# Graph attention layer in the tail: the last octet's scores and softmax earlier, the last iteration's pooling and decoding a step earlier in another PSUM bank

## The reference

```python
h = x @ w_lin + b_lin
dense[n, pos] = h[src of edge]                        # n x 32 x 64, mask[n, pos]
xb = mab(dense, dense, enc_*, mask)                   # attention, + residual, + relu(ff)
xp = relu(xb @ pma_lin_w + pma_lin_b)
p  = mab(seed, xp, pma_*, mask)                       # one query a node
dd = mab(p, p, dec_*)
out = relu(nan_to_num(dd))
return layernorm(x + out)
```

## Time and profile before

| | |
|---|---|
| time, median of 3 runs | 4012.61 us (4012.59 to 4014.58) |
| the profiled execution | 4014.11 us, span 4012.3 us |
| busy PE, DVE, POOL, ACT | 78%, 76%, 74%, 41% of the span |
| mean granted clock of TensorE | 0.923 |
| last gather issued | 3948.2 to 3949.2 us |
| last instruction ends | 4012.3 us |

### The profile page before, as it was taken

One profiled execution on the slowest core, in us unless ns is written; L12 is line 12 of the kernel. 1 busy time (PEld: TensorE's weight loads), 2 busy tenths in 40 slices (PEclk: granted clock), 3 DMA queues, 4 the chain that ended last, 5 costly groups with the idle time before them and its releaser, 6 DMA issues.

```text
span 4012.3 us, 111968 instructions
## 1 busy us (share of the span) xinstructions
PE 3111.6 (78%) x30804; PEld 2000.9 (50%) x30804; DVE 3057.7 (76%) x7192; ACT 1663.4 (41%) x3006; POOL 2979.5 (74%) x3145
## 2 busy tenths in 40 slices
PE   7877887877777778777787787787877777877777
PEld 5544554554545445545454455454554554545443
DVE  6877877877778768777787787777877877778876
ACT  3443443444434434444444344344444443434443
POOL 6777777777777777777777777777777777777772
PEclk8999998999989989999899899998999999999898
DMA  6333333333333333333333333333333333333331
GB/s 215 90 90 90 90 91 90 90 91 89 90 90 89 91 90 89 90 90 90 90 89 90 90 89 91 90 90 90 89 91 90 90 90 90 90 90 89 87 109 34
DMA packets 186843, 369.25 MB, mean 92 GB/s; under 512 B 66610, under 2 KB 119002, under 8 KB 186090
## 3 DMA queue, kind: packets, MB, share of 16 engines
q0 software_dynamic: 150080, 307.11, 28.8%
q1 hardware_dynamic: 29802, 45.03, 3.5%
q10 hardware_dynamic: 6208, 8.40, 0.7%
HBM read 347.48 MB, written 16.32 MB: 91 GB/s over the span
## 4 chain that ended last, share of the span: by engine, by line
POOL 66%; issue 24%; PE 6%; DVE 2%; DMA 1%; POOLq 1%; SPq 0%; ACT 0%; DVEq 0%
POOL gathered L620 66%; DMA gathered<-node_table,idx 1%; PE ps L788 1%; PE ps L726 1%; PE ps L738 1%; PE ps L770 1%; PE ps L801 0%; DVE windows L1135 0%; PE ps L815 0%; PE ps L831 0%; PE ps L762 0%; POOLq L131 0%; DMA node_table<-gathered 0%; PE ps L689 0%; DVE probs_diag L1382 0%
## 5 line engine op out<-in xcount | busy, mean ns | idle before, releaser
L620 POOL DMA_INDIRECT gathered<-node_table,idx x3093 | 2934.4, 949 | 943.3 <-issue 938.7
L726 PE MATMUL ps<-ident,gathered 128*128 128x128 f32 x3128 | 583.5, 315 | 458.2 <-DMA gathered<-node_table,idx 452.3
L726 PEld LDWEIGHTS ps<-ident,gathered 128*128 128x128 f32 x3128 | 485.1, 203 | 796.0 <-issue 732.2
L852 ACT ACTIVATE h_apart<-ps 64x512 f32<-64x512 f32 x782 | 462.3, 591 | 448.9 <-PE ps L726 355.3
L925 ACT ACTIVATE qT<-ps,cols 128x512 f32<-128x512 f32 x391 | 268.8, 687 | 854.3 <-PE ps L726 754.4
L1306 DVE SCALAR_TENSOR_TENSOR xb<-ps,cols,h 128x512 f32<-128x512 f32 x391 | 292.1, 747 | 417.6 <-PE ps L788 412.4
L1382 DVE STREAM_TRANSPOSE probs_diag<-probs 32x512 f32<-32x512 f32 x784 | 549.0, 700 | 18.4
L738 PE MATMUL ps<-probs_diag,gathered 128*64 128x128 f32 x6256 | 462.4, 292 | 107.4 <-issue 106.1
L788 PE MATMUL ps<-h,ff_diag 128*128 128x512 f32 x782 | 484.0, 705 | 76.0 <-DVE h L1262 75.5
L738 PEld LDWEIGHTS ps<-probs_diag,gathered 128*64 128x64 f32 x6256 | 373.9, 169 | 276.8 <-issue 259.1
L852 ACT ACTIVATE xp_rows<-ps 128x512 f32<-128x512 f32 x391 | 233.4, 597 | 601.0 <-PE ps L762 419.6
(11 more groups left out here) (205 smaller groups left out, 3287.2 us busy)
## 6 DMA issues: line engine op xcount, KB each, us to landing
windows<-win_table SPq DMA_DIRECT2D x8960, 2.8 KB
gathered<-node_table,idx POOLq DMA_INDIRECT x3093
windows<-win_table ACTq DMA_DIRECT2D x2944, 2.8 KB
node_table<-gathered SPq DMA_DIRECT2D x24, 384.0 KB, 2.8
out_rows<-rows SPq DMA_DIRECT2D x5, 416.0 KB
win_table<-in_dst SPq DMA_DIRECT2D x1, 1716.0 KB
win_table<-in_src SPq DMA_DIRECT2D x1, 1716.0 KB
rows<-in_x SPq DMA_DIRECT2D x2, 640.0 KB, 5.1
```

Source lines behind the costliest of these rows:

```text
L620: pool.indirect_dma_start(out=gathered[:, s.slot(0, RING), t * ROW:(t + 1) * ROW], out_offset=None, in_=table, in_offset=bass.IndirectOffs ...
L726: mm = pe.transpose(ps[:, bank, p * P:(p + 1) * P], gathered[:, s.slot(0, RING), lo:lo + 2 * ROW - 2:3], ident[:, :])
L852: return nc.scalar.activation(o, i, ACT.Copy)
```

## The change

`alone()` is true in step 391 of the written-out tail, `alone(1)` in 392, `alone(2)` in 393. In step 391 the scores of batch 195 are issued directly behind attend(387) on PE instead of at the end of the step. DVE's mask, add, maximum and difference of that batch move from step 392 to step 391, behind the second half of the transposes and ahead of the statistics; ACT's exp moves from the end of 392 to the end of 391; the share-out and the transposes move from step 393 to step 392. For iteration 97 alone, everything from the seed mask to y is a step sooner in program order (395 to 402 instead of 396 to 403), and its transposed weights, pooling and decoding results are in bank B_Q, which the turn of an octet used before; its pooling has no wait for `y_ok` then. The looped steps and all other written-out steps have the same instructions in the same order. The same code of the batch's softmax now stands in functions (`masked`, `shared_out`, `from_top`, `first_half`).

```diff
+LAST_SOONER = {L_SEED: 1, L_SEED_T: 1, L_WEIGHTS: 1, L_POOL: 1, L_DEC1: 1, L_DEC2: 1, L_OUT: 1, L_Y: 1}
...
+    def sooner(self, lag):
+
+        if self.looped or lag not in LAST_SOONER:
+            return 0
+        last = (self.octets - 1) // 4 * 4
+        return LAST_SOONER[lag] if self.at - lag + LAST_SOONER[lag] == last else 0
...
-        return self.group * (PERIOD // 4) + (self.at - lag) // 4
+        return self.group * (PERIOD // 4) + (self.at - lag + self.sooner(lag)) // 4
...
+    def alone(self, after=0):
+        return not self.looped and self.at == self.octets + after
+
     def has_iteration(self, lag):
-        return (self.at - lag) % 4 == 0 and (self.looped or 0 <= self.at - lag < self.octets)
+        at = self.at - lag + self.sooner(lag)
+        if at % 4 or self.looped:
+            return at % 4 == 0
+        moved = LAST_SOONER.get(lag, 0) and at == (self.octets - 1) // 4 * 4 and not self.sooner(lag)
+        return 0 <= at < self.octets and not moved
...
+        def pool_bank(s, lag):
+            return B_Q if not s.looped and s.iteration(lag) == ITS - 1 else B_POOL
+
+        def seedT_of(s, lag):
+            return ps[:, pool_bank(s, lag), P:2 * P]
+
+        def fin_of(s, lag):
+            return ps[:, pool_bank(s, lag), 2 * P:3 * P]
...
                     mm.then_inc(av_ps, 1)
+                if s.alone():
+                    scores(s)
                 if s.has_iteration(L_DEC1):
-                    fin_op(s, L_DEC1, pooled_ok, ps_fin[0:D, :], pooled, ident)
+                    fin_op(s, L_DEC1, pooled_ok, fin_of(s, L_DEC1)[0:D, :], pooled, ident)
...
                     wait(pe, weights2_ok, s.iteration(L_POOL) + 1)
-                    wait(pe, y_ok, s.iteration(L_POOL))
+                    if pool_bank(s, L_POOL) == B_POOL:
+                        wait(pe, y_ok, s.iteration(L_POOL))
...
-                        mm = pe.matmul(ps[DEG * c:DEG * c + DEG, B_POOL, :],
+                        mm = pe.matmul(ps[DEG * c:DEG * c + DEG, pool_bank(s, L_POOL), :],
...
-                if s.has_batch(L_SCORES):
...
+                if s.has_batch(L_SCORES) and not s.alone():
+                    scores(s)
+
+            def scores(s):
+                wait(pe, p_norm, s.batch(L_SCORES))
+                wait(pe, q_sb, s.octet(L_SCORES - 2))
+                wait_apart(pe, h_parted, s.octet(L_SCORES - 2) * 2, pe_passed)
...
-                if s.has_batch(L_SOFTMAX):
-                    wait(act, s_diff, s.batch(L_SOFTMAX) + 1)
+                if s.alone() or s.has_batch(L_SOFTMAX) and not s.alone(1):
+                    wait(act, s_diff, s.batch(L_SOFTMAX - s.alone()) + 1)
                     nc.scalar.activation(ps_scores, ps_scores, ACT.Exp).then_inc(p_exp, 1)
...
+                if s.has_batch(L_SOFTMAX) and not s.alone(1):
+                    masked(s, L_SOFTMAX)
+                if s.has_batch(L_NORM) and not s.alone(2):
+                    shared_out(s, L_NORM)
+                if s.alone(1):
+                    shared_out(s, L_NORM - 1)
                 if s.has(L_H2):
...
+                if s.has_batch(L_SOFTMAX) and not s.alone(1):
+                    from_top(s, L_SOFTMAX)
+                if s.has_batch(L_NORM) and not s.alone(2):
+                    first_half(s, L_NORM)
+                if s.alone(1):
+                    first_half(s, L_NORM - 1)
...
-                if s.has_batch(L_NORM):
-                    to_diagonal(s, pr, QUADS // 2, QUADS)
+                if s.has_batch(L_NORM) and not s.alone(2):
+                    to_diagonal(s, L_NORM, QUADS // 2, QUADS)
+                if s.alone(1):
+                    to_diagonal(s, L_NORM - 1, QUADS // 2, QUADS)
+                if s.alone():
+                    masked(s, L_SOFTMAX - 1)
+                    from_top(s, L_SOFTMAX - 1)
                 if s.has_iteration(L_Y):
                     y_stats(s)
```

More of the change, by code:

```diff
@@ L1227, in step @@
                     y_rows(s)
[L1228 to L1243, removed]
@@ L1291, in step @@
                     wait(dve, fin_ps, m * 6 + 3)
-                    V.scalar_tensor_tensor(pvec[:, :], ps_fin[0:D, :], c_("bff2"), hid1[:, :], ALU.add, ALU.max
+                    V.scalar_tensor_tensor(pvec[:, :], fin_of(s, L_DEC2)[0:D, :], c_("bff2"), hid1[:, :], ALU.add, ALU.max
                                            ).then_inc(pvec_ok, 1)
@@ L1377, in step, with masked @@
                     act_rows_of(s)
-            def to_diagonal(s, pr, first, last):
+            def masked(s, lag):
+                n = s.batch(lag)
+                dve.wait_ge(s_ps, n + 1)
+                V.tensor_tensor(
+                    empty[:, :].rearrange("p (o t j) -> p o t j", o=2, j=DEG),
+                    ps_iota.unsqueeze(1).unsqueeze(1).broadcast_to((P, 2, OCT, DEG)),
+                    count_slot[:, bass.ds(n * 16, 16)].rearrange("p (o t) -> p o t", o=2).unsqueeze(3).broadcast_to(
+                        (P, 2, OCT, DEG)), ALU.is_ge).then_inc(mask_ok, 1)
+                if s.has_iteration(lag):
+                    m = s.iteration(lag)
+                    V.tensor_copy(count_seed[:, bass.ds(m, 1), :].rearrange("p m a -> p (m a)"), ps_counts[:, 0:QUADS])
+                    V.tensor_scalar(nonempty[:, bass.ds(m, 1)], ps_counts[:, QUADS:QUADS + 1], 0.0, None, ALU.is_gt
+                                    ).then_inc(counts_read, 1)
+                dve.wait_ge(mask_ok, n + 1)
+                V.scalar_tensor_tensor(ps_scores, empty[:, :].rearrange("p (h n) -> p h n", h=2), MASKED, ps_scores,
+                                       ALU.mult, ALU.add).then_inc(s_sb, 1)
@@ new lines, in shared_out @@
+            def shared_out(s, lag):
+                pr = probs[:, s.slot(lag, 4) // 2, :]
+                n = s.batch(lag)
+                dve.wait_ge(p_exp, n + 1)
+                V.tensor_reduce(total[:, :].rearrange("p (h t) -> p h t", h=2), ps_slots, AX_X, ALU.add
+                                ).then_inc(p_sum, 1)
+                dve.wait_ge(p_sum, n + 1)
+                V.reciprocal(share[:, :], total[:, :]).then_inc(p_share, 1)
+                dve.wait_ge(p_share, n + 1)
+                V.tensor_tensor(pr.rearrange("p (h t j) -> p h t j", h=2, j=DEG), ps_slots,
+                                share[:, :].rearrange("p (h t) -> p h t", h=2).unsqueeze(3).broadcast_to(
+                                    (P, 2, OCT, DEG)), ALU.mult).then_inc(p_norm, 1)
@@ L1380, in to_diagonal, with first_half @@
+            def first_half(s, lag):
+                n = s.batch(lag)
+                dve.wait_ge(p_norm, n + 1)
+                wait(dve, av_ps, s.octet(lag + 2))
+                to_diagonal(s, lag, 0, QUADS // 2)
+            def to_diagonal(s, lag, first, last):
+                pr = probs[:, s.slot(lag, 4) // 2, :]
                 for q in range(first, last):
                     lo = DEG * q
-                    V.transpose(probs_diag[lo:lo + DEG, s.slot(L_NORM, 4) // 2, :, lo:lo + DEG],
+                    V.transpose(probs_diag[lo:lo + DEG, s.slot(lag, 4) // 2, :, lo:lo + DEG],
```

75 lines of the change are left out of this document (39 added, 36 removed).

## The result

The changed kernel takes 4019.87 us (median of 22 runs, 4016.16 to 4022.9), the kernel before 4013.68 beside it (22 runs, 4011.7 to 4017.46). The ratio is 1.0016, with a 95% interval of 1.001 to 1.0021: 6.2 us slower, where 3.3 were forecast. It is within the 0.2% that was taken for no change, and 0.4 us above the upper end of the stated range.

What follows compares the result with a forecast made beforehand. Bound: POOL's pace of issuing gathers in the loop, DVE's queue in the tail. Order 3.5, plus clock 1.4, less decode 1.65, is 3.3 us slower: 4015.9 us against the median 4012.61, range 4010.5 to 4019.5.

Steps and rivals of the forecast that it cites:

- Scores in step 391, "1.83 late": Step 391 on PE: the moved scores wait for the norm and hold up back and seed; ff(387) starts 1.83 us late.
- PE's idle stretch of 3.6 us, DEC1 4.5 late: Step 392 on PE: first decoding transpose waits for DVE's pooling until 3970.40, 4.5 us later; PE idles 3.6.
- What sets ff(388): Step 392: PE has back and seed done at 3972.08 but waits for h2; ff(388) starts at 3972.77.
- The order costs 3.5 at the full clock: Steps 391 to 394: xb(388) 4.88 us late, 1.35 back in steps 393 and 394, so 3.5 lost.
- That adds 1.4 us; ... so no more is added.: Behind PE's 3.6 us wait: clock falls for 5.6 us, slowing back, seed and ff; 1.4 us more.
- the stated bound of 2.9: Upper bound of the clock term in steps 392 and 393: 2.9 us if pma and attend are still slow.
- rival of a later recovery: Step 393: clock returns one step later, pma, attend and part of back slow, another 1.5 to 2.5 us, 4018; 13%.
- Part 2, 1.65 back: Last decode: pooling(97) follows the OUT matmul without waiting for y of 96, winning 1.65 us; bounds 0 to 2.2.
- The detour: Decode of iteration 96: transpose of seed weights and its product stand ahead of pvec, costing 0.47 us together.
- The sum: Whole tail: 3.5 for the order plus 1.4 for the clock less 1.65 for the decode, 3.3 us slower.
- Different time up to the last gather: Ahead of the tail: a sign that the prediction is wrong, putting the cause outside the tail; no size given.

Runs made afterwards that it cites:

- e14: Changed kernel with unused extra matmuls filling both PE waits (four in step 391, seven in 392), third run: 1.7 us over before, ratio 1.0005.
- e6: Changed kernel, but in step 391 DVE does the pooling of iteration 95 ahead of the moved softmax instructions: ratio 1.0001 against before.
- e5: Changed kernel with unused extra matmuls filling both PE waits (four in step 391, seven in 392), first run: ratio 1.0003 against before.
- e4: The changed kernel again, unaltered, for a second trace: ratio 1.0007 against before.
- e9: The changed kernel again, unaltered, for a third trace: ratio 1.0004 against before.
- e2: Kernel before with only the scores and softmax of the last batch moved, iteration 97 and its bank as before: ratio 1.0011 against before.
- e8: Kernel before with only the scores and softmax of the last batch moved, second run: ratio 1.0006 against before.
- e16: The changed kernel again, unaltered, for a fourth trace: 5.2 us over before, ratio 1.0013.
- e3: Changed kernel with eleven unused extra matmuls in step 392, filling only PE's second wait, ahead of DEC1: ratio 1.0013 against before.
- e1: Kernel before with only iteration 97 a step sooner and in the other bank, softmax as before: ratio 0.9996 against before.
- e7: Kernel before with only iteration 97 a step sooner and in the other bank, second run: ratio 0.9986 against before.
- e10: Changed kernel with unused extra matmuls filling both PE waits (four in step 391, seven in 392), second run: ratio 0.9998 against before.
- e15: Softmax as before, iteration 97 a step sooner in the other bank, its pooling two steps sooner, second run: 4.1 us below before, ratio 0.999.

## Why the prediction was right in direction and short in size

- **Scores in step 391, "1.83 late".** Right: ff(387) is 5.88 behind attend(387), before 4.03, 1.85 late.
- **PE's idle stretch of 3.6 us, DEC1 4.5 late.** Right: 3.55 in the changed kernel's first trace, the transpose 4.53 late.
- **What sets ff(388).** The text put PE's idle stretch in bold; its own sum then let ff(388) wait for h2, by 0.7. The sum was right, and the idle stretch by itself costs nothing at the full clock: with the clock up, ff(388) waits 0.63 for h2 (e14), and e6, which releases DEC1 2.8 earlier, has h2(388) no earlier.
- **The order costs 3.5 at the full clock.** Right: 29.83 less 26.38 is 3.45 (e5). xb(388) is 4.92 late (e14), where 4.88 was forecast, and steps 393 and 394 give back 1.48, where it was 1.35: xb to xb is 6.05 and 6.17.
- **The step that failed: "That adds 1.4 us; ... so no more is added."** The fall behind the second wait was rightly foreseen. Its size was taken from one low stretch, put at 5.6 us behind a restart (5.8 by the 0.77 of the earlier trace rows), and only waits of 3.5 us and more were looked at. The runs show three things in its place. First, the term is 1.56, 5.05, 5.16 and 4.67 in four traces (the time to xb(390) less 29.83), so the stated bound of 2.9 was too low. Second, the wait of 2.15 that the moved scores make can bring a fall too, and the prediction gave it no price: of eight traces with that wait the clock is down ahead of the scores in two (e4, e9), falls within them in three (e2, e6, e8) and just behind them in one (e16), and stays up in two (the first trace, e3). Third, the second stretch ends 5.0 to 5.2 us behind the restart in three traces (the first, e2, e8), but 8.7 to 11.6 behind it in four (e4, e6, e9, e16), over pma(388) and attend(389). The rival of a later recovery (13%) came closest, with 4018.
- **The trace of before could have warned.** From 3000 to 3950 it has 18 waits of 2.0 to 3.1 us for gathered rows. Behind 11 of them the next ff takes 1.02, behind the 7 others 1.42 to 1.92. One of each:

```profile
3217.47 1.09 PE L726 MATMUL ps<-ident,gathered 128*128 128x128 f32 x4 [2.41 <-DMA gathered<-node_table,idx]
3218.36 1.91 PE L788 MATMUL ps<-h,ff_diag 128*128 128x512 f32 x2
...
3944.78 0.69 PE L726 MATMUL ps<-ident,gathered 128*128 128x128 f32 x4 [2.38 <-DMA gathered<-node_table,idx]
3945.31 1.02 PE L788 MATMUL ps<-h,ff_diag 128*128 128x512 f32 x2
```

- **Part 2, 1.65 back.** Measured 1.0 to 1.1 in e1 and e7, 1.1 to 1.5 in the changed kernel. The detour itself was rightly priced for the full clock. From the first matmul of DEC2 to pvec it was 0.47 (3991.47 to 3991.94), and in e10, where the clock is still up, it is 0.93, 0.46 more:

```profile
6466.05 0.43 PE L878 MATMUL ps<-hid,p_ff 64*64 64x128 f32 x2 [0.45 <-ACT hid L941]
...
6466.98 0.33 DVE L1294 SCALAR_TENSOR_TENSOR pvec<-ps,cols,hid 64x128 f32<-64x128 f32 x1
```

What was off is again the clock. In the first trace it is down ahead of that matmul and the same way takes 1.33 (3996.15 to 3997.48), 0.86 more. Every trace has a fall in the decode of 96 that lasts to the end, and its place matters: it comes 9.1 us behind xb(390) in before, e4 and e9, where the gain is 1.5, and 7.9 to 8.1 behind it in e1, e7 and the first trace, where it is 1.0 to 1.3.

- **The sum.** 3.45 + 1.56 - 1.26 = 3.75 in the trace that was taken of the result, and 3.45 + 5.0 - 1.4 = about 7.0 in the three others. A median of 6.2 over 22 runs is what a mixture of these would give; the two traces on such chips have tails of 59.63 and 62.90 and times of 4017.77 and 4021.02, 3.3 apart in both. e14 and e16 show in times that it is the clock. How often each case occurs I can't say from four traces.
- **"Different time up to the last gather".** Not seen: attend(387) starts at 3956.42 and 3953.83 in the two traces of before and at 3955.97 and 3955.90 in the two of the changed kernel on chips of this speed. By so few a difference of 1 us there can't be excluded.

The Trainium skill ("TensorE: Matmul & The Clock Gate", "HAM oscillation — how this bites in real kernels") counts the loss of a matmul engine that is left waiting twice: the waits themselves, and apart from them what runs cold behind. The second part is borne out here by e14 against e16: 3.5 us.

## What to carry to other kernels

When a tail is bound by one engine's queue, work that is moved forward in program order starts sooner only by making something else wait: here the scores start 3.27 behind attend(387) instead of 7.12, and h2(388) 15.47 instead of 10.65. Price the queue of the engine that is full (here DVE), then look at what the new waits do to TensorE's clock, over the whole chain behind them and not over one group, and for the short waits as well as the long ones. Where a term depends on the clock, a single profile shows one draw of it; the range has to hold several low stretches. And ask of a last iteration which of two interleaved chains ends the kernel, and let that one go first (e15).

## What the runs showed that was not expected

Extra matmuls with no use made the changed kernel faster by 3.5 us (e14 against e16). The clock fell behind a wait of 2.15 us in six of eight traces, and not in the two others; what decides between them was not found. Two chips ran the same kernel at 6488 to 6530 us instead of 4013, with a granted clock of 0.75 on the mean instead of 0.92; the tail had the same lengths there, so the loss is ahead of it. In the loop PE's matmuls of the scores waited 28.9 us for "issue", that is, for nothing that the profile shows, in the 100 us from 3000 of e9. What makes those waits was not tried.
